# Reloads in pairs: SyncE issues both stores of a unit, then both reloads of the unit before

## The reference

```python
def _L0_conv_ref(x, weight, bias):
    x_cat = jnp.concatenate([x, x[:, :, :-1, :]], axis=2)
    out = jax.lax.conv_general_dilated(x_cat, weight, window_strides=(1, 1), padding='VALID',
        dimension_numbers=('NCHW', 'OIHW', 'NCHW'), feature_group_count=x.shape[1])
    return out + bias[None, :, None, None]
...
x = x + _L0_conv_ref(_gn(x), L0_conv_weight, L0_conv_bias)
```

## Time and profile before

| | |
|---|---|
| median of three runs | 825.06 us (818.1 to 828.1) |
| profiled execution | 822.96 us, span 820.9 us |
| PE / DVE / ACT / POOL busy | 86% / 87% / 86% / 71% |
| DMA queue q1, share of 16 engines | 99.0% |
| moved | 333.82 MB, mean 407 GB/s |
| load of a half, issue to landing | 15.6 us median |
| store of a half, issue to landing | 17.6 us median |

### The profile page before, as it was taken

How to read it: one execution, slowest core, us unless ns; L and a number is a source line. 1 busy time by engine, 2 the same in 40 slices (tenths; PEclk the granted TensorE clock), 3 DMA queues, 4 the chain that set the end, 5 groups by cost and what they waited for, 6 DMA issues and landing times.

```text
span 820.9 us, 8753 instructions
## 1 busy us (share of the span) xinstructions
PE 703.0 (86%) x1920; PEld 561.1 (68%) x1920; DVE 710.6 (87%) x1588; ACT 705.5 (86%) x1153; POOL 580.4 (71%) x1114
## 2 busy tenths in 40 slices
PE   0779989888998998898888889888899888988896
PEld 0557767777776776777767777676677665776785
DVE  7889989999998998989889988888898878888883
ACT  2679999999999998898999998898998887889983
POOL 3467777777777777767767777766777766676776
PEclk9989999999999999999999999999999999999998
DMA  8999999999999999999999999999999999999967
GB/s 349 417 382 382 405 413 421 424 420 417 423 425 423 426 419 423 426 427 428 428 427 428 426 429 428 427 427 426 427 421 415 412 395 408 406 399 399 386 230 272
DMA packets 36548, 333.82 MB, mean 407 GB/s; under 512 B 4624, under 2 KB 4752, under 8 KB 5776
## 3 DMA queue, kind: packets, MB, share of 16 engines
q1 hardware_dynamic: 36496, 333.27, 99.0%
HBM read 179.11 MB, written 154.14 MB: 406 GB/s over the span
## 4 chain that ended last, share of the span: by engine, by line
DMA 41%; ACT 22%; issue 13%; PE 8%; DVE 8%; POOL 7%; SPq 0%; POOLq 0%; ACTq 0%
DMA out<-xt 18%; DMA xt<-x 14%; ACT xn L428 10%; DMA runs<-taps 8%; PE conv L542 7%; ACT kept L456 7%; DVE st L317 5%; ACT xn L433 4%; POOL xt L275 2%; DVE xt L353 2%; POOL newt L267 1%; POOL newt L266 1%; POOL rstd L268 1%; POOL shift L269 1%; POOL newt L265 1%
## 5 line engine op out<-in xcount | busy, mean ns | idle before, releaser
L542 PE MATMUL conv<-xn,runs 128*128 128x448 f32 x1536 | 661.1, 577 | 41.4 <-ACT xn L428 29.9
L542 PEld LDWEIGHTS conv<-xn,runs 128*128 128x128 f32 x1536 | 514.8, 346 | 114.0 <-ACT xn L428 45.2
L275 POOL TENSOR_TENSOR xt<-xt,kept 128x448 f32<-128x448 f32 x384 | 434.6, 1139 | 168.9 <-ACT kept L456 168.8
L317 DVE BATCH_NORM_STATS2 st<-xt 128x6 f32<-128x336 f32 x1024 | 451.5, 494 | 37.6 <-DMA xt<-x 36.0
L428 ACT ACTIVATE xn<-xt,shift,rstd 128x672 f32<-128x672 f32 x463 | 418.8, 942 | 45.3 <-POOL shift L269 43.9
L353 DVE SCALAR_TENSOR_TENSOR xt<-conv,bias_all,xt 128x448 f32<-128x448 f32 x384 | 257.1, 670 | 18.0 <-PE conv L542 17.5
L456 ACT ACTIVATE kept<-conv,bias_all 128x448 f32<-128x448 f32 x384 | 235.2, 622 | 13.4 <-PE conv L542 12.6
L515 PEld LDWEIGHTS p_mean<-msum,neg_mean 128*128 128x128 f32 x128 | 21.2, 201 | 97.0 <-POOL msum L244 80.6
L515 PE MATMUL p_mean<-msum,neg_mean 128*128 128x8 f32 x128 | 25.1, 268 | 61.0 <-POOL msum L244 61.0
L433 ACT ACTIVATE xn<-xt,shift,rstd 128x336 f32<-128x336 f32 x80 | 47.4, 660 | 3.4 <-POOL shift L269 3.3
L523 PEld LDWEIGHTS p_var<-st,avg 128*128 128x128 f32 x128 | 20.6, 195 | 40.3 <-POOL dev L258 37.6
(11 more groups left out here) (35 smaller groups left out, 147.7 us busy)
## 6 DMA issues: line engine op xcount, KB each, us to landing
xt<-x SPq DMA_DIRECT2D x128, 1344.0 KB, 15.6
out<-xt SPq DMA_DIRECT2D x128, 1176.0 KB, 17.6
runs<-taps SPq DMA_DIRECT2D x32, 84.0 KB, 16.7
bias_all<-bias SPq DMA_DIRECT2D x1, 192.0 KB, 13.7
```

Source lines behind the costliest of these rows:

```text
L275: nc.gpsimd.tensor_tensor(cell, cell, kept_of(u, c), ALU.add).then_inc(pool_added, 1)
L317: ins = nc.vector.bn_stats(st[:, n % RS, h, b, :], xt[0:P, slot(n, h), b * ROW:(b + 1) * ROW])
L542: nc.tensor.matmul(bank(c), lay[:, :, c], xn_of(u, c), start=True, stop=True).then_inc(conv_ready, 1)
```

## The change

From half 5 on, SyncE no longer follows each store by one reload. After the first store of a unit it goes on to the second; after that it issues two reloads, of the slots of the two halves of the unit before (at half 5 the one reload of slot 3, for half 16). Reloads, their waits and their slots are the same as before, and so is all else.

```diff
                     k = HALVES * u + h
                     if 1 <= k < HEAD:
                         load(k - 1 + XH)
-                    if k > HEAD:
-                        load(k - 2 + XH)
+
+                    if k >= HEAD and h == 1:
+                        for j in range(max(HEAD - 1, k - 3), k - 1):
+                            load(j + XH)
```

## The result

The changed kernel took 875.55 us in the median of five runs (867.36 to 881.24), the kernel before 828.1 us in five runs beside them. The ratio is 1.060, with a 95% interval of 1.054 to 1.065. The forecast was 829 us, no measurable change; its range, 817 to 843, missed by 33 us. Ratios in this text are of executions outside a second, slower state that some executions of each kernel are in; medians are of all runs.

What follows compares the result with a forecast made beforehand. The prediction took the DMA transfers to bound the kernel. Order term 1.9, early queue term 2.4 and steady queue term 1.9 summed to 6.2 us on the profiled 822.96, so 829 us, range 817 to 843.

Steps and rivals of the forecast that it cites:

- What bounds it: Whole kernel: transfers are the bound, so the change is priced by their rate and when the last load lands.
- The walk of the steady unit: One unit from a moved load's landing: stores land after 14.9 and 11.8 us, moved load after 15.0; queue never empty.
- The queue terms: Shorter time in the queue lowers the rate: 2.4 us early (82 to 205 us), 1.9 us steady (287 to 600 us).
- The order term: End of run: the last load goes behind one more store, a shift paid once, 1.9 us (1.0 to 2.82).
- Only the order counts: Rival for the whole run: the queue terms are nothing, time 825 us; chance 0.27.
- The Trainium skill's rule: Any queue: a DMA costs about 2 us fixed beside its bytes, so cover over some 2 us would hide everything.
- Leading engines run dry: Rival, early and from 287 us on: thinner cover lets leading DMA engines find the queue empty; 848 us, chance 0.15.
- faster: Rival: runs of like transfers go better, the late stretch (615 to 779 us) returns to 427 GB/s; 815.7 us, chance 0.10.
- The Trainium skill's ceiling of 435 GB/s: Steady stretch: the fabric ceiling, by which order could gain at most 5.8 us over 313 us.

Runs made afterwards that it cites:

- xh12: The kernel before with 12 slots in place of 13, order unchanged; ratio 1.000 (0.993 to 1.006).
- d_store: Transfers alone, no compute: 13 halves loaded once, then 128 stores of 112 partitions back to back, no reloads or waits; 534.17 us.
- d_ssll4: d_ssll with the two reloads being of the unit stored two units ago, so some 24 us of transfers stay queued; 852.29 us.
- d_sl1: d_sl2 with the reload of the slot stored one half ago instead of two; 851.15 us.
- d_ssll: d_sl2 in the order of the change: two stores, then the two reloads of the unit stored before; 859.97 us.
- d_sl2: The transfers alone, without compute, taps or bias, in the order and with the waits of the kernel before; 798.13 us.
- d_store128: d_store with stores of all 128 partitions into a scratch tensor; 471.11 us.
- d_store10: d_store with stores of only 40 partitions, so 10 of the 16 engines carry four packets of each; 473.43 us.
- lag3: The kernel before, still alternating, with each reload of the slot stored three halves ago instead of two; 857.8 us in the median of four runs, no ratio.
- mid: The order of the change for units 0 to 31, that of the kernel before from unit 32 on; ratio 1.035 (1.028 to 1.041).
- d_sl3: d_sl2 with the reload of the slot stored three halves ago; 792.92 us.
- fine: The kernel before with each store and reload cut in two along the free dimension, parts in turn; ratio 1.009 (1.005 to 1.013).

## Why the prediction was wrong

**What bounds it: right.** Transfers did, and their rate decided. The measured 875.55 us lies beyond the range of 817 to 843.

**The walk of the steady unit: wrong in its times.** It had stores landing after 14.9 and 11.8 us and moved loads after 15.0. Measured in 320 to 600 us were 16.5 in the median (12.8 to 20.9) and, for all loads, 18.9. The walk charged 2.82 us for every store. In a pair the second takes more: among stores alone one takes 3.6.

**The queue terms: the step that failed.** They priced the length of the queue, and the price of a store behind a store was put at nothing. "Up to 600 us a longer queue goes with a higher rate. This table is what the forecast rests on." In the earlier trace rows length and rate did rise together, but one did not make the other. xh12 has the queue of the forecast, 13.3 us, and 424 GB/s; the change has 16.5 us and 398. The terms were 2.4 and 1.9 us, the measured losses 15 us up to 287 and 20 from 320 to 600. I had priced a store by bytes over the mixed rate, and looked for no row with stores alone. There was one, taken for something else: the last stretch, with share 0.74 and a store that took over 14 us to land, holds stores only. Its 253 GB/s at a share of 0.74 are 342 at a full one, against 427 in the mix, and its packets took 505 ns against 406. That price would have given the result: an estimate with 3.63 us, from d_store's slower run, makes one store of each of 62 pairs 0.81 us longer, 50 us in all, where 47 were measured between the medians and 44 between the profiled executions; a unit becomes 12.26 + 0.81 = 13.07 us, where 13.0 was measured.

**The order term: not separable.** DVE waits 3.2 us for the last load where it waited 1.0; what the one store more ahead of it adds cannot be told from the slower queue. That the middle of its bounds was taken, as half of the full price in both queue terms, had no row behind it. DVE's timeline of the changed kernel:

```profile
823.88 1.33 DVE L319 BATCH_NORM_STATS2 st<-xt 128x6 f32<-128x336 f32 x3 [3.23 <-DMA xt<-x]
```

**"Only the order counts" (0.27)** is ruled out: it gave 825. The Trainium skill's rule that was cited for it is given for DMAs issued from GpSimd, by the section's own title, and these are SyncE's; cover was not what decided in either case.

**"Leading engines run dry" (0.15)** gave 848 and a rate of 403 to the end, nearest in size, and its sign, 13.0 us a unit, came true; but by luck, for its mechanism was wrong. A thinner cover was not what did it (xh12), a cover of some 24 us did not cure it (d_ssll4), and no engine ran dry: the share is 0.99 to 1.01 wherever d_sl1, d_ssll and, from 123 us to 656, the changed kernel lose rate.

**The "faster" rival** (0.10) took runs of like transfers for an advantage; they are the cost.

**The Trainium skill's ceiling of 435 GB/s** was not reached (the best rates here are 429 to 431) and asked how much order could gain; how much it could lose was the question.

What was shown: the pair order as such costs (d_ssll against d_sl2), through stores behind stores (d_store), whose packets take longer, and only with the stores of 112 partitions (d_store128, d_ssll128). That engines meet at a port is inferred: from the two kinds of packet and their count in d_store10, and for the stores of 112 from less. Not settled: whether load packets are slow too in the changed kernel (the traces don't tell them from a store's); what makes packets slow in an alternating order, in lag3, in d_sl1, in mid's profiled execution after the switch and in the kernel before from 615 us on, though d_sl3 has none. All would fit an alternation that is fast only while the 16 engines are spread so that about half of them store at any time, but no run sets that spread.

## What to carry to other kernels

Before you regroup transfers, time each kind alone with a full queue: a rate of a mix can hide that one kind is slow when it meets its own. Look first in the stretch at the end, where only stores are left. A store of fewer than 128 partitions is worth such a test, since it may make the order of the queue matter. And a rise of rate with queue length over one trace is no price for queue length: one run with one slot less (xh12) showed that.

## What the runs showed of the hardware that was not expected

- Stores of 112 partitions back to back ran at 332 GB/s, of 128 partitions at 423, loads at 425. With each other in turn, stores of 112 and loads ran at 427 to 429 in the transfers alone (d_sl2, d_sl3), and at 395 and 396 in the profiled executions of lag3 and mid.
- There are two kinds of packet in d_store10, near 404 and near 828 ns, for the same 10,752 bytes.
- The DMA share reads 0.99 to 1.01 at 332 GB/s and at 429 alike: it does not show that packets are slow.
- With packets of half the size (fine) the best slices show 423 GB/s, where full-size ones reach 429.
